# A fused four-layer block: exponential before copy in ScalarE's order of the first attention layer

## The chip, the cores and the metric

One Trainium2 chip, one of its cores. A core has TensorE (matmuls, into the PSUM banks), VectorE, ScalarE and GpSimd (elementwise work; ScalarE has the exponential), and SyncE, which here only issues transfers. Each engine works off its own list of instructions in order and waits at semaphores for the others. The metric is the device time of one execution of the whole kernel in microseconds (us); lower is better. Three runs of a kernel give a median.

## The reference, cut to what matters

The whole function is a block of four layers over x of 32 sequences x 128 tokens x 128 features, each an attention layer and a feed-forward layer with a gated residual. The change touches the first attention layer alone, which has 16 query heads of 8 features and values shared in groups:

```python
def _L0_xattn_ref(x, adj, Wq, bq, Wk, bk, Wv, bv, Wo, bo):
    q = x @ Wq + bq
    k = adj @ Wk + bk
    v = adj @ Wv + bv
    q = q.reshape(b, t, N_HEADS, D_HEAD).transpose(0, 2, 1, 3)
    k = k.reshape(b, v_len, GROUP, D_HEAD).transpose(0, 2, 1, 3)
    v = v.reshape(b, v_len, GROUP, D_HEAD).transpose(0, 2, 1, 3)
    weight = jnp.einsum('bhtd,bgvd->bhtv', q, k) / math.sqrt(D_HEAD)
    weight = jax.nn.softmax(weight, axis=-1)
    out = jnp.einsum('bhtv,bgvd->bhtd', weight, v)
    out = out.transpose(0, 2, 1, 3).reshape(b, t, N_HIDDEN)
    return out @ Wo + bo
...
x = x + jnp.tanh(g_xattn[0]) * _L0_xattn_ref(_layernorm(x, axis=-1), ctx_1024, ...)
```

## The kernel before, in words

The 32 sequences go through a layer in 8 chunks of 4 (`NC = 8`, `CB = 4`). In the first attention layer (`heads0`, one function of that name in each engine's program) a chunk is 8 steps (`STEPS0`), w = 0 to 7. A step takes one unit: 8 (head, sequence) score blocks of 128 x 128, that is two PSUM banks. The order of each engine's instructions is written out by hand: each engine's `body(c, p, more, first, live)` loops over the steps and emits, at fixed lags (`LAG0`), the work of this unit and of earlier ones. Nothing reorders it; semaphores alone tie the engines together.

What happens to unit v, and in which step each engine does it:

- TensorE, step v: scores into banks 0 and 1 (L918). It waits until VectorE has read the scores of the unit before (`A0_less_max`).
- VectorE, step v: the maximum of each row (L2075), then scores minus maximum into the buffer `ex` (L2078, tile `att`), which counts up `A0_less_max`. `ex` has two halves, taken in turn.
- ScalarE, step v: the exponential in place in `ex` (shown as L1485), which counts up `A0_exp`. It waits for `A0_less_max`.
- TensorE, step v+1: eight transposes of `ex` into banks 2 and 3 (L947), which count up `A0_pT_full`. They wait for the exponential and, as there is one pair of banks, for the copy of unit v-1 (`A0_pT`).
- ScalarE, step v+1: the copy of banks 2 and 3 into `pT0` (128x1024, shown as L1483 with tile `arena`), which counts up `A0_pT`. `pT0` holds four units.
- TensorE, in odd steps: the values matmul (L929) of the tile of two units of which the second is v = w-2. It stands after the scores and before the transposes. It waits for `A0_pT` of both units and for `A0_oT`, that is for a small copy (`oT0`, 128x128) that ScalarE makes in even steps behind the big one.
- Then, for the tile: ScalarE copies the result (`outT0`, 128x512, at the end of even steps), TensorE transposes it back (L971), VectorE divides by the sums (L2086, L2087), TensorE transposes again (L936), ScalarE copies to `oT0`, TensorE projects (L961, odd steps), and VectorE adds the residual once a chunk (L2127, step 5).

Beside this the queries, keys and values of the next chunk are prepared in eight pieces (`piece`, `SLICES0 = (0, 0, 1, 4, 5, 6, 6, 7)` gives the step of each). TensorE makes a piece in one PSUM bank, ScalarE copies it out and gives the bank free (`A0_slice_gone`). A step's first piece stands early in the step on both engines (on ScalarE ahead of all else), a second one (steps 0 and 6) late. GpSimd splits keys and queries into bf16 parts in between (L641 to L645).

ScalarE's step before the change is thus: first piece, copy of unit w-1 to `pT0`, copy to `oT0` (even steps), second piece, exponential of unit w, copy to `outT0` (even steps).

The first chunk is followed by a setup of weights for later layers on all engines; chunks 1 to 4 run in a hardware loop, 5 to 7 are written out, and six steps of draining follow chunk 7, which has no pieces (there is no next chunk). The first layer's feed-forward part begins in the drain.

Of the kernel before, what the change touches and what calls it, by code (L numbers as in the profile page):

```python
# [30 lines left out]
STEPS0 = 2 * CB  # L31
# [35 lines left out]
CRED = QUARTERS + 1  # L67
# [42 lines left out]
def slices_at(w):  # L110

    return [s for s, at in enumerate(SLICES0) if at == w]
# [12 lines left out]
def lagging(c, p, w, what, first, live):  # L125

    lag = LAG0[what]
    if w >= lag:
        return (c, p, w - lag) if live else None
    return None if first else (c - 1, 1 - p, w - lag + STEPS0)  # L130


def tile_of(unit, odd=0):

    return (unit[0], unit[1], unit[2] // 2) if unit and unit[2] % 2 == odd else None


def flamingo(nc, a, out):
    ctx = ExitStack()
    with ctx:  # L140
# [5 lines left out]
        def sem(name):  # L146
            if name not in sems:
                sems[name] = ctx.enter_context(nc.semaphore(name))
            return sems[name]
# [7 lines left out]
        def two(i):  # L157
            return banks[:, i:i + 2, :].rearrange("p a (j t) -> p (a j) t", j=CB)

        def slice_bank(s, first):  # L160
            return bank[(6 - s) % 8] if first else bank[6]
# [28 lines left out]
        ex = att[:, 0:2].rearrange("p a s j t -> p (a s) j t")  # L190
# [179 lines left out]
        at = used[0]  # L370
# [1111 lines left out]
        def _(act):  # L1482
            copy = lambda o, i: nc.scalar.activation(o, i, ACT.Copy)  # L1483
            aff = lambda o, i, s, b: nc.scalar.activation(o, i, ACT.Identity, bias=b, scale=s)
            exp = lambda o, i: nc.scalar.activation(o, i, ACT.Exp)  # L1485
            s_held = sem("held")

            def setup():
                act.wait_ge(s_load, 16 * n_loads)
                nc.scalar.activation(gates[:, :], graw[:, :], ACT.Tanh).then_inc(s_setup, 1)  # L1490
# [20 lines left out]
            def heads0():  # L1511
                kA = len(SLICES0)

                def piece(c, p, s, first=False):
                    A = slice_bank(s, first)
                    A16 = A[:, :].bitcast(BF16)
                    act.wait_ge(sem("A0_slice"), c * kA + (s + 1))
                    gone = sem("A0_slice_gone")
                    if s == 0:
                        copy(xnT[:, :], A[:, :]).then_inc(sem("A0_xnT"), 1)  # L1520
                        act.wait_ge(sem("A0_xnT"), c + 1)
                        act.sem_inc(gone, 1)
                        return
                    if s < 3:

                        if s == 1:
                            copy(kvraw0[:, :, :], A[:, 0:CB * KV0].rearrange("p (j d) -> p j d", j=CB)).then_inc(sem("A0_raw"), 1)
                        else:
                            nc.scalar.activation(qraw0[:, :, :], A[:, :].rearrange("p (h d) -> p h d", d=D0), ACT.Copy, scale=float(D0) ** -0.5)\
                                .then_inc(sem("A0_raw"), 1)  # L1530
                        act.wait_ge(sem("A0_raw"), c * 2 + s)
                        act.sem_inc(gone, 1)
                        return
                    if s == 3:
                        for q in range(2):
                            half = slice(q * (P // 2), (q + 1) * (P // 2))
                            i = copy(kT0[half, p, :, q * P:q * P + P], A16[half, 0:W].rearrange("p (j t) -> p j t", j=CB))
                    else:
                        i = copy(qT0[:, p, s - 4, :], A16[:, :])
                    i.then_inc(gone, 1)  # L1540
                    if s == kA - 1:
                        act.wait_ge(gone, c * kA + (kA + 1))
                        act.sem_inc(sem("A0_slices_ready"), 1)

                def body(c, p, more, first=False, live=True):
                    for w in range(STEPS0 if live else DRAIN0):
                        mine = slices_at(w) if more else []
                        for s in mine[:1]:
                            piece(c + 1, 1 - p, s)
                        unit = lagging(c, p, w, "turned", first, live)  # L1550
                        if unit:
                            cc, _, v = unit
                            act.wait_ge(sem("A0_pT_full"), cc * STEPS0 + (v + 1))
                            act.wait_ge(sem("A0_pv_batch"), cc * CB + (v // 2 + 1))
                            at = 2 * v % PT0
                            copy(pT0[:, at:at + 2, :, :].rearrange("p a i t -> p (a i) t"), two(2)).then_inc(sem("A0_pT"), 1)
                        tile = tile_of(lagging(c, p, w, "attended", first, live))
                        if tile:
                            cc, _, j = tile
                            act.wait_ge(sem("A0_oT_full"), cc * (2 * CB) + (2 * j + 2))  # L1560
                            copy(oT0[:, j % 2, :], bank[4 + j % 2][:, 0:P]).then_inc(sem("A0_oT"), 1)
                        for s in mine[1:]:
                            piece(c + 1, 1 - p, s)
                        if live:
                            act.wait_ge(sem("A0_less_max"), c * STEPS0 + (w + 1 + CRED))
                            at = ex[:, w % 2 * 2:w % 2 * 2 + 2, :, :].rearrange("p a i t -> p (a i) t")
                            exp(at, at).then_inc(sem("A0_exp"), 1)
                        tile = tile_of(lagging(c, p, w, "copied", first, live))
                        if tile:
                            cc, _, j = tile  # L1570
                            act.wait_ge(sem("A0_pv_batch"), cc * CB + (j + 3))
                            if j or not isinstance(cc, int) or cc:
                                act.wait_ge(sem("A0_oT_full"), cc * (2 * CB) + (2 * j - 1))
                            copy(outT0[:, :], bank[4 + j % 2][:, :]).then_inc(sem("A0_out"), 1)

                act.sem_inc(sem("A0_slice_gone"), 1)
                act.sem_inc(sem("A0_pT"), CRED)
                act.sem_inc(sem("A0_exp"), CRED)
                act.sem_inc(sem("A0_pv_batch"), 2)
                act.sem_inc(sem("A0_oT"), 2)  # L1580
                for s in range(kA):
                    piece(0, 0, s, first=True)
                body(0, 0, True, True)
                setup()
                with act.Fori(0, NC // 2 - 2) as i:
                    for p in range(2):
                        body(i * 2 + (p + 1), 1 - p, True)
                body(NC - 3, 1, True)
                body(NC - 2, 0, True)
                body(NC - 1, 1, False)  # L1590
                body(NC, 0, False, live=False)
# [1114 lines left out]
```

## Time and profile before

| what | before |
|---|---|
| median of 3 runs | 1580.54 us (1576.93 to 1581.98) |
| profiled execution: its own time, which is its span | 1593.7 us |
| TensorE matmuls busy | 1390.0 us (87%) |
| VectorE busy | 1102.3 us (69%) |
| ScalarE busy | 1016.4 us (64%) |
| mean granted TensorE clock | 0.960 |

The profiled execution is one execution with the profiler on, and the times within it are read from its first instruction. The first attention layer lies between about 35 and 280 us of it. Busy shares are means over a span in which stages with different limits follow each other; what holds for the stage of the change is read from its own stretch.

### The profile page before, as it was taken

To read this page: it belongs to the slowest core of one execution; us is meant where nothing else is said; L and a number is where in the kernel's file an instruction comes from. 1 tells how busy PE (TensorE), PEld (TensorE's weight loads), DVE (VectorE), ACT (ScalarE), POOL (GpSimd) and SP (SyncE) were. 2 spreads that over 40 slices of the span, in tenths; PEclk is the share of its full clock that TensorE was granted. 3 is DMA by queue.
4 is the path that set the end of the run, shared out by engine and by line. 5 is a ranking of instruction groups with operands and counts; after the bars stand their busy time and mean duration, and the time that the engine had idled before them with its cause. 6 is when DMAs were issued, how large, how long until landed. Compare 5 with 4: busy or idle time off the path is not lost.

```text
span 1593.7 us, 35101 instructions
## 1 busy us (share of the span) xinstructions
PE 1390.0 (87%) x9982; PEld 1034.7 (65%) x9982; DVE 1102.3 (69%) x3531; ACT 1016.4 (64%) x2931; POOL 533.7 (33%) x631
## 2 busy tenths in 40 slices
PE   4788887998898987998999989999986299999994
PEld 3566665676644465443666666666665299999994
DVE  4788877787777666884567767777675556666665
ACT  2688886554555564224887867877864277777762
POOL 3353566222211411000002242342243445554550
PEclk9999999999999999999999999999998599999998
DMA  8000059400499910000000010010034122222227
GB/s 194 24 8 7 14 93 178 69 0 14 96 179 179 136 34 21 0 0 7 1 8 23 13 36 18 18 34 11 18 133 156 37 62 66 67 66 65 63 57 264
DMA packets 143417, 98.35 MB, mean 62 GB/s; under 512 B 20595, under 2 KB 132510, under 8 KB 142150
## 3 DMA queue, kind: packets, MB, share of 16 engines
q1 hardware_dynamic: 134598, 80.08, 25.2%
q0 software_dynamic: 8704, 16.87, 3.2%
q8 instruction: 55, 0.90, 0.2%
q14 instruction: 60, 0.49, 0.1%
HBM read 43.03 MB, written 54.93 MB: 61 GB/s over the span
## 4 chain that ended last, share of the span: by engine, by line
PE 59%; DVE 13%; ACT 12%; issue 11%; another core or an unknown queue 2%; DMA 1%; DVEq 1%; SPq 1%; POOL 0%; ACTq 0%; POOLq 0%
PE bank L1450 7%; PE bank L1442 7%; PE bank L1006 6%; PE bank L1022 4%; ACT arena L1483 3%; PE bank L947 3%; PE bank L1294 3%; PE bank L1057 3%; ACT att L1620 3%; PE bank L1010 2%; PE bank L1042 2%; ACT att L1485 2%; PE bank L1032 2%; PE bank L1370 2%
## 5 line engine op out<-in xcount | busy, mean ns | idle before, releaser
L1483 ACT ACTIVATE arena<-bank 128x512 f32<-128x512 f32 (+7 forms) x380 | 245.6, 675 | 150.4 <-PE bank L1357 53.9
L1902 ACT ACTIVATE att<-bank,arena 128x128 f32<-128x128 f32 x576 | 165.0, 371 | 70.0 <-PE bank L1442 65.8
L820 POOL DMA_INDIRECT expert_outputs<-arena x144 | 145.1, 1007 | 146.6 <-issue 100.8
L1620 ACT ACTIVATE att<-bank,arena 128x128 f32<-128x128 f32 x512 | 180.7, 395 | 17.1 <-DVE arena L2160 14.6
L774 POOL DMA_INDIRECT dispatched_rows<-arena x112 | 113.8, 1016 | 181.2 <-DVE arena L2049 115.3
L608 POOL TENSOR_TENSOR ve<-mv,eps 128x4 f32<-128x4 f32 x64 | 13.0, 203 | 425.9 <-DVE mv L1965 416.9
L1450 PE MATMUL bank<-arena,att 128*128 128x128 f32 x1152 | 153.5, 276 | 2.3 <-ACT att L1902 1.7
L1442 PE MATMUL bank<-xnT,arena 128*128 128x128 f32 x1152 | 154.0, 277 | 0.4 <-ACT xnT L1483 0.4
L1450 PEld LDWEIGHTS bank<-arena,att 128*128 128x128 f32 x1152 | 140.1, 192 | 4.8 <-ACT att L1902 4.8
L1442 PEld LDWEIGHTS bank<-xnT,arena 128*128 128x128 f32 x1152 | 141.6, 194 | 1.0 <-ACT xnT L1483 1.0
L1483 ACT ACTIVATE xnT<-bank 128x128 f32<-128x128 f32 (+1 forms) x180 | 63.5, 353 | 90.9 <-PE bank L841 43.1
L1620 ACT ACTIVATION_READ_ACCUMULATOR att<-bank,arena 128x1 f32 x512 | 120.2, 235 | 0.0
L2632 DVE COPY arena<-arena 128x512 f32 x144 | 62.3, 433 | 82.9 <-issue 81.6
L2160 DVE TENSOR_REDUCE arena<-bank 128x4 f32<-128x512 f32 x128 | 82.3, 685 | 45.4 <-PE bank L1022 45.3
L1605 ACT ACTIVATE arena<-bank 128x512 f32<-128x512 f32 x128 | 76.0, 613 | 58.1 <-PE bank L1006 50.8
L947 PE MATMUL bank<-ident,att 128*128 128x128 f32 x512 | 70.9, 283 | 31.7 <-ACT att L1485 31.5
L1022 PE MATMUL bank<-arena 64*128 64x128 f32 x1024 | 79.7, 292 | 18.3 <-issue 7.4
L2075 DVE TENSOR_REDUCE nmx<-bank 128x8 f32<-128x1024 f32 x64 | 78.0, 1219 | 25.4 <-PE bank L918 24.9
L2174 DVE COPY arena<-bank 128x512 f32<-128x512 f32 x64 | 44.0, 687 | 72.4 <-PE bank L1042 38.1
L1022 PEld LDWEIGHTS bank<-arena 64*128 64x128 f32 x1024 | 66.5, 193 | 40.6 <-issue 31.6
L2166 DVE TENSOR_TENSOR att<-att,arena 128x512 f32<-128x512 f32 x128 | 89.0, 695 | 4.4
L1294 PE MATMUL bank<-arena 128*128 128x512 f32 x192 | 89.4, 603 | 0.0
(375 smaller groups left out, 3257.0 us busy)
## 6 DMA issues: line engine op xcount, KB each, us to landing
dispatched_rows<-padf SPq DMA_DIRECT2D x16, 2128.5 KB, 31.8
arena<-dispatched_rows SPq DMA_DIRECT2D x144, 64.5 KB
cxT<-in_ctx SPq DMA_DIRECT2D x32, 256.0 KB
arena<-in_L_ffn_w SPq DMA_DIRECT2D x8, 1024.0 KB
arena<-expert_outputs SPq DMA_DIRECT2D x8, 1024.0 KB, 13.8
expert_outputs<-arena POOLq DMA_INDIRECT x144
out_x<-x SPq DMA_DIRECT2D x8, 256.0 KB, 4.9
dispatched_rows<-arena POOLq DMA_INDIRECT x112
```

What stands on the lines that cost most here:

```text
L774: pl.indirect_dma_start(sent, bass.IndirectOffsetOnAxis(places[:, q:q + 1], 0), held[:, q, :], None)\
L820: pl.indirect_dma_start(sent_out, bass.IndirectOffsetOnAxis(xtu3[:, s, P:P + 1], 0), yt3[:, s, :], None, bounds_check=TOP3 * TOKENS - 1, o ...
L947: last = nc.tensor.transpose(bank[2 + k][:, i * P:i * P + P], ex[:, v % 2 * 2 + k, i, :], ident[:, :])
L1006: last = nc.tensor.matmul(A[:, :], wqk3[:, t, pair * P:pair * P + P], cxT[:, p, :] if t else xnT[:, :], start=True, stop=True)
L1022: last = nc.tensor.matmul(bank[side][:, i * P:i * P + P], q, k, start=True, stop=True)
L1294: last = nc.tensor.matmul(bank[1 + j][:, :], xsT1[:, p * CB + j, t:t + P], wconv1[:, t, :], start=False, stop=(t == 2))
L1442: last = nc.tensor.matmul(bank[s % 2][:, k * P:k * P + P], w1c3[:, s % 4, k * P:k * P + P], xnT[:, (s % 4) * P:(s % 4) * P + P], start=Tru ...
L1450: last = nc.tensor.matmul(bank[2 + s % 2][:, 0:P], h3[:, s % 2, k * P:k * P + P], w2c3[:, s % 4, k * P:k * P + P], start=(k == 0), stop=(k ...
L1483: copy = lambda o, i: nc.scalar.activation(o, i, ACT.Copy)
L1620: last = nc.scalar.activation(ex3_of(w, side)[:, i, :], bank[side][:, i * P:i * P + P], ACT.Exp, bias=nm3[:, w % 2, h:h + 1], accum_out=su ...
L1902: last = nc.scalar.activation(h3[:, s % 2, k * P:k * P + P], bank[s % 2][:, k * P:k * P + P], ACT.Gelu, bias=b1c3[:, s % 4, k:k + 1])
L2166: v.tensor_tensor(ex3_of(w, side), ex3_of(w, side), rs3[:, w % 2, side:2 * HQ:2].unsqueeze(2).to_broadcast([P, HQ, P]), ALU.mult) .then_in ...
```

## The change

In ScalarE's `body` of `heads0` the exponential of unit w goes from behind the second piece to directly behind the first piece, ahead of the copy of unit w-1. Its wait for VectorE goes with it. Nothing else is touched. ScalarE's step is then: first piece, exponential of unit w, copy of unit w-1 to `pT0`, copy to `oT0` (even steps), second piece, copy to `outT0` (even steps).

```diff
                         for s in mine[:1]:
                             piece(c + 1, 1 - p, s)
+                        if live:
+                            act.wait_ge(sem("A0_less_max"), c * STEPS0 + (w + 1 + CRED))
+                            at = ex[:, w % 2 * 2:w % 2 * 2 + 2, :, :].rearrange("p a i t -> p (a i) t")
+                            exp(at, at).then_inc(sem("A0_exp"), 1)
                         unit = lagging(c, p, w, "turned", first, live)
                         if unit:
...
                         for s in mine[1:]:
                             piece(c + 1, 1 - p, s)
-                        if live:
-                            act.wait_ge(sem("A0_less_max"), c * STEPS0 + (w + 1 + CRED))
-                            at = ex[:, w % 2 * 2:w % 2 * 2 + 2, :, :].rearrange("p a i t -> p (a i) t")
-                            exp(at, at).then_inc(sem("A0_exp"), 1)
                         tile = tile_of(lagging(c, p, w, "copied", first, live))
```

## Rows read from the trace of the kernel before

**Rows 1.** The page, part 5: the group of the transposes of unit v

```profile
L947 PE MATMUL bank<-ident,att 128*128 128x128 f32 x512 | 70.9, 283 | 31.7 <-ACT att L1485 31.5
```

**Rows 2.** Busy time by stretch: a loaded chunk, and the setup

```profile
core 0: us, PE busy (x) PEld busy (x) DVE busy (x) ACT busy (x) POOL busy (x), PEclk, DMA share, GB/s
129.04:158.29 29.25, 24.49 (x214) 18.18 (x215) 24.00 (x38) 24.59 (x34) 14.20 (x14) 1.00 0.03 9
62.00:72.00 10.00, 6.48 (x33) 5.98 (x33) 7.34 (x20) 2.24 (x6) 0.00 (x0) 0.66 0.00 0
```

**Rows 3.** Timeline of one loaded chunk: start us, us, engine, line, tiles, count

```profile
129.42 1.22 DVE L2078 TENSOR_TENSOR att<-bank,nmx 128x1024 f32<-128x1024 f32 x1
...
131.78 1.07 PE L929 MATMUL bank<-arena 128*32 128x512 f32 x8
...
134.65 0.39 PE L961 MATMUL bank<-wo,arena 128*128 128x128 f32 x2
...
134.87 0.60 PE L918 MATMUL bank<-arena 128*128 128x256 bf16 x4
...
136.77 1.23 DVE L2078 TENSOR_TENSOR att<-bank,nmx 128x1024 f32<-128x1024 f32 x1
...
136.95 1.09 PE L947 MATMUL bank<-ident,att 128*128 128x128 f32 x8 [1.37 <-ACT att L1485]
...
138.08 1.19 ACT L1483 ACTIVATE arena<-bank 128x1024 f32<-128x1024 f32 x2 [1.18 <-PE bank L947]
...
139.16 1.06 ACT L1485 ACTIVATE att<-att 128x1024 f32<-128x1024 f32 x1
...
139.32 1.07 PE L929 MATMUL bank<-arena 128*32 128x512 f32 x8 [0.41 <-ACT arena L1483]
...
140.32 1.09 PE L947 MATMUL bank<-ident,att 128*128 128x128 f32 x8
...
141.25 0.39 PE L961 MATMUL bank<-wo,arena 128*128 128x128 f32 x2
...
141.55 0.61 PE L918 MATMUL bank<-arena 128*128 128x256 bf16 x4
...
142.45 1.05 ACT L1485 ACTIVATE att<-att 128x1024 f32<-128x1024 f32 x1
143.40 2.48 ACT L1483 ACTIVATE arena<-bank 64x512 bf16<-64x512 bf16 x4
143.46 1.22 DVE L2078 TENSOR_TENSOR att<-bank,nmx 128x1024 f32<-128x1024 f32 x1
...
145.92 1.07 PE L929 MATMUL bank<-arena 128*32 128x512 f32 x8 [0.41 <-ACT arena L1483]
...
150.73 1.23 DVE L2078 TENSOR_TENSOR att<-bank,nmx 128x1024 f32<-128x1024 f32 x1
...
152.89 1.07 PE L929 MATMUL bank<-arena 128*32 128x512 f32 x8
...
153.88 0.45 PEld L903 LDWEIGHTS bank<-ident,arena 128*128 128x128 bf16 x8 [0.84 <-ACT arena L1483]
...
154.75 1.09 PE L947 MATMUL bank<-ident,att 128*128 128x128 f32 x8 [0.24 <-ACT att L1485]
...
158.74 1.22 DVE L2078 TENSOR_TENSOR att<-bank,nmx 128x1024 f32<-128x1024 f32 x1
```

**Rows 4.** Timeline of chunk 7, which has no pieces

```profile
246.47 1.23 DVE L2078 TENSOR_TENSOR att<-bank,nmx 128x1024 f32<-128x1024 f32 x1
...
266.06 1.22 DVE L2078 TENSOR_TENSOR att<-bank,nmx 128x1024 f32<-128x1024 f32 x1
...
272.56 0.86 PEld L947 LDWEIGHTS bank<-ident,att 128*128 128x128 f32 x8 [1.10 <-ACT att L1485]
```

**Rows 5.** Timeline of chunk 0 and the start of chunk 1

```profile
41.44 1.22 DVE L2078 TENSOR_TENSOR att<-bank,nmx 128x1024 f32<-128x1024 f32 x1
...
54.21 1.22 DVE L2078 TENSOR_TENSOR att<-bank,nmx 128x1024 f32<-128x1024 f32 x1
...
71.38 1.23 DVE L2078 TENSOR_TENSOR att<-bank,nmx 128x1024 f32<-128x1024 f32 x1
...
73.20 1.06 PE L929 MATMUL bank<-arena 128*32 128x512 f32 x8
```

## Prediction

> **What bounds the kernel now.** I read the page first, then the stretches, then the timeline of one chunk, engine against engine. The page's costliest groups name one wait of this stage: TensorE's transposes of the probabilities (L947) stood 31.7 us idle, 31.5 of it for the exponential [rows 1]. So the exponential is the last thing before the transposes. The reader is to see next that no engine is full: in a chunk of 29.25 us TensorE is busy 24.5, VectorE 24.0 and ScalarE 24.6 us, at a granted clock of 1.00 [rows 2]. The stage is therefore bound by chains that go from engine to engine, and the question is which chains pass through ScalarE's order.
>
> I call M(w) the moment at which VectorE has subtracted the maximum in step w (end of L2078), T(w) the eight transposes of unit w, which TensorE issues in its step w+1, and PV the values matmul (L929), which stands in TensorE's queue in odd steps between the scores and T. Two loops run side by side in the timeline [rows 3]. The first: T(w-1), copy, exponential, T(w). In the step after 136.95 that is 1.09 for T, 0.04, copy to exponential 1.08 (138.08 to 139.16, with the small copy of oT0 behind it) and 1.06 for the exponential. The second: scores 0.60, maximum, subtraction 1.22, next scores, since the scores may overwrite their banks only after M. They are of one length. M(2) is 136.77 + 1.23 = 138.00, and the transposes beside it end at 136.95 + 1.09 = 138.04. ScalarE takes the copy at 138.08 and the exponential at 139.16; both inputs were there at 138.0 in truth. From that instant ScalarE has two pieces of work, and the change only swaps them.
>
> **What each one releases.** T(w) needs both: the exponential as its input, the copy because it writes the banks that the copy reads. For T(w) it doesn't matter which comes first. PV needs the copy alone (and in these steps the small copy of oT0, which follows it), and PV is ahead of T in TensorE's queue. Today PV runs while ScalarE does the exponential: it starts at 139.32, T at 140.32 the moment it has been issued. After the change ScalarE's copy comes second, PV starts only after both, and its 1.00 us and all that is queued behind it (piece, T, projection, the next scores, VectorE's maximum and subtraction) come later. That is a wait added to the path that sets the stage's period.
>
> **The price of one pair of steps.** After M of an even step: release 0.04 (138.04 to 138.08), exponential 0.95 (142.45 to 143.40, start to start), the big copy and that of oT0 together 1.19 (138.08, x2), release 0.05 (139.27 to PV at 139.32). PV starts 2.23 after M. Where it starts now, all from [rows 3]:
> - steps 0 and 1: M at 129.42 + 1.22 = 130.64, PV 131.78, 1.14 behind; the chain behind it is TensorE's queue, then scores, maximum, subtraction. Later by 1.09.
> - steps 2 and 3: M 138.00, PV 139.32, 1.32 behind; 0.91 later. The scores behind it waited a little for VectorE: they follow the projection by 0.22 elsewhere (134.65, 134.87), by 0.30 here (141.25, 141.55), so 0.08 is absorbed. Later by 0.83.
> - steps 4 and 5: M 143.46 + 1.22 = 144.68, PV 145.92, 1.24 behind. Later by 0.99.
> - steps 6 and 7: M 150.73 + 1.23 = 151.96, PV 152.89. Here the next piece waited 0.84 for another copy of ScalarE's (153.89), and T came at 154.75, 2.79 behind M. In the new order that copy follows the one of oT0 and ends about 3.1 behind M, under PV, which is through after its 1.00 at 3.23; the piece takes 0.45, T comes at 3.68. Later by 0.89.
>
> Together 3.80 us a chunk: 29.25 becomes about 33.05. The six chunks 1 to 6 make 22.8.
>
> **The edges.** Chunk 7 carries no pieces of a next chunk. Its three pairs from 246.47 to 266.06 take 19.59 [rows 4]. A bare pair comes out in the new order as 2.23 + 1.00 (PV) + 1.15 (T and the projection up to the scores: 140.32 to 141.47 without the 0.08) + 0.60 + 2.53 (scores' end to M: 134.87 + 0.60 to 138.00) = 7.51, the third with some 0.35 for the residual, which waits for the projection: 22.9, or 3.3 more. The last T (272.56, 5.28 behind M(6)) needs both results after the copy of outT0 and comes some 0.6 later. Chunk 0: two pairs between 41.44 and 54.21 take 12.77 [rows 5]; without projection and, at first, without oT0 the new pairs are about 7.1 and 7.5: 1.8 more. Its last pair runs into the setup, for which ScalarE has to finish the same two pieces in either order: nothing. In chunk 1, M(0) is 71.38 + 1.23 = 72.61 and PV 73.20, just 0.59 behind, since the copy had been made during the setup: 0.55 more than counted. Sum: 22.8 + 3.9 + 1.8 + 0.55 = 29.0 us.
>
> **What is moved, and what is queued behind it.** No instruction is added, removed or resized, and none of those moved issues a DMA. The exponential's wait for VectorE now stands ahead of the big copy, the copy of oT0 and, in steps 0 and 6, the second piece's copy. Behind them wait PV, the next T (banks 2 and 3), the projection, the pieces of TensorE that need the slice bank free, and through PV GpSimd's split of the next chunk's keys and queries. That split ends early enough: its queries are wanted at step 5, in a chunk that is itself 3.8 us longer. SP's loads of the context wait for a TensorE piece and are used one chunk later. Where the trace shows no such order the bounds are these: below, a gain if M comes well ahead of the end of T (next part); above, 2.23 - 0.59 = 1.64 for each of the 31 PVs concerned (0.59 being the earliest place of PV in the rows [rows 5]), 51 us. I take the sum, since each term is read at its own place in a chunk.
>
> **A rule weighed.** The rows say that TensorE's transposes are kept waiting by the exponential, 31.5 us in all [rows 1]. By that alone, an exponential issued first should win. The Trainium skill says so in general: Perfetto Trace Analysis, section "Identifying Performance Opportunities" (Optimization Strategy), finds the gaps of the bounding engine, asks which semaphore ends them, and has that dependency start sooner. Applied to this wait it speaks for the change, and would bring the time of the first rival below. The trace does not bear it out here, because what is put off in exchange releases the same engine.
>
> **The rivals.**
> 1. Faster: the exponential hides under the transposes. If M(w) came at least 0.95 before T(w-1) ended, ScalarE would do the exponential during T, and T's loop would be 1.09 + 0.04 + 1.02 + 0.04 = 2.2 us; the scores and VectorE's loop would bound, about 2 us a chunk less: 1580.5 - 16 = 1565. It decides at that lead. The lead is 0.04 at M(2) [rows 3]. Chance 0.04.
> 2. No change, 1578 to 1584: PV's delay is eaten by slack. This needs under 0.15 us per PV where I count 0.83 to 1.09; the slack that I find is 0.08. Chance 0.04.
> 3. Half the loss: the exponential, done earlier, lets loaded steps (copies of pieces) catch up by some 0.4 per pair, 31 x 0.45 = 14: 1594, at most 1600. For it: ScalarE is idle 4.7 us of 29.25. Chance 0.11.
> 4. Larger: even steps lose too, because ScalarE, standing at the exponential, takes up the copy late when VectorE runs behind T (maximum late by the residual or the norm). Some 0.45 more per step over 56 steps: +54, 1635. Against it: M and the end of T lie 0.04 apart in the step shown, and a late M delays the next scores in either order. Chance 0.06.
> 5. The clock falls. With setup's idle TensorE the granted clock was 0.66 over ten microseconds [rows 2], which is a mix of the 2.4 and the 1.2 GHz level. If the longer waits did that to this stage, PV, T, projection and scores of each pair (about 2.7 us) would double: 31 x 2.7 more, about 1693. Waits such as the 1.37 ahead of T at 136.95 [rows 3] stand in a chunk at 1.00 today; the new ones are some 1.6 us. Chance 0.03. The Trainium skill has such a rule (TensorE: Matmul & The Clock Gate, section "HAM oscillation"): idle gaps put the engine back to half rate; no run here yet shows it for gaps of this size.
>
> **How the numbers follow.** The profiled execution's own time is its span, 1593.7 us; the timed runs have a median of 1580.5, 13.2 below, and the difference lies around the stage, not in it. So the span should be about 1622.7, and the median 1580.5 + 29.0 = 1609.5. Forecast 0.72. Its own range is 1603 to 1615: plus or minus a fifth of the sum. To leave out no more than two in ten, the range goes down to 1596, into the third rival, and up to 1618; the far cases 1, 2, 4 and 5 stay outside. About 0.3%, some 5 us, is what a measurement of this kernel can tell from no change. Faster 0.04 (rival 1), same 0.04 (rival 2), slower 0.92 (the others).
>
> **What would show it.** In the changed profile the exponential starts within 0.1 us of the end of L2078's subtraction and the idle time before it is put down to VectorE. The wait of PV for ScalarE's copy grows to over 1 us in nearly every odd step; T in odd steps no longer waits for the exponential but stands right behind PV or its piece. A chunk lasts 33 us, a bare pair 7.5 us. The waits of VectorE's maximum for the scores grow by about the same sum. The granted clock stays 1.00 and everything after the first attention layer is only shifted. I am wrong if PV does not wait longer, if the exponential often ends before T does, or if the chunk is under 31 us.

## The result, and the profile after

The changed kernel takes 1615.81 us (median of 5 runs, 1611.49 to 1617.82); the kernel before, run beside it, 1580.26 us (1576.93 to 1581.98). The ratio is 1.0218, with a 95% interval of 1.0201 to 1.0236: slower by 35.5 us. The forecast was 1609.5 in a range of 1596 to 1618.

The profiled execution of the changed kernel has a span of 1611.8 us, that of the kernel before 1593.7. These two spans must not be subtracted. I take as the layer's end the first matmul with the gate weights of the feed-forward part (L1118). It stands here in the trace of before:

```profile
282.20 1.84 PE L1118 MATMUL bank<-xnT,wg 128*128 128x512 f32 x2
```

and here after the change:

```profile
314.82 2.05 PE L1118 MATMUL bank<-xnT,wg 128*128 128x512 f32 x2
```

From there to the end the execution of before took 1311.5 us, the changed one 1297.0, and the executions of the experiments below 1291 to 1298 with the same code in that part. The profiled execution of before was a long one, by 15 us, in stages that the change does not touch. What can be compared is the layer: its end moved from 282.20 to 314.82, by 32.6 us.

Groups by line, from 30 to 320 us of the changed kernel; the columns are count, busy us and mean ns, then idle time of the engine ahead of them and what ended it. L947 are the transposes T, L1485 is the exponential, L929 the values matmul PV:

```profile
L947 PE MATMUL bank<-ident,att 128*128 128x128 f32 x512 | 69.8, 281 | 26.0 <-ACT arena L1483 26.0
L1485 ACT ACTIVATE att<-att 128x1024 f32<-128x1024 f32 x64 | 67.5, 1055 | 38.3 <-DVE att L2078 36.3 <-ACT arena L1483 0.7 <-ACT arena L1529 0.4
...
L929 PE MATMUL bank<-arena 128*32 128x512 f32 x256 | 35.0, 617 | 44.6 <-ACT arena L1483 44.6
```

The same view of the kernel before, for the two lines not shown there yet (T is in [rows 1]):

```profile
L1485 ACT ACTIVATE att<-att 128x1024 f32<-128x1024 f32 x64 | 67.5, 1055 | 1.9 <-DVE att L2078 1.1 <-ACT arena L1483 0.2
...
L929 PE MATMUL bank<-arena 128*32 128x512 f32 x256 | 34.1, 603 | 8.4 <-ACT arena L1483 8.2
```

Three readings. PV waited 8.2 us for ScalarE's copy (tile `arena`, L1483) and now waits 44.6. The exponential, which waited for nothing (1.9), now stands 36.3 us at VectorE's subtraction, that is at the head of ScalarE's list with the copy behind it. T waited 31.5 us for the exponential and now 26.0 for the copy, which has become the second of the two: the wait that the swap removes comes back under another name.

The timeline of one loaded chunk of the changed kernel, which answers to [rows 3]:

```profile
141.75 1.22 DVE L2078 TENSOR_TENSOR att<-bank,nmx 128x1024 f32<-128x1024 f32 x1
...
143.01 1.06 ACT L1485 ACTIVATE att<-att 128x1024 f32<-128x1024 f32 x1 [1.33 <-DVE att L2078]
...
143.98 1.29 ACT L1483 ACTIVATE arena<-bank 128x1024 f32<-128x1024 f32 x3
...
145.20 1.06 PE L929 MATMUL bank<-arena 128*32 128x512 f32 x8 [1.15 <-ACT arena L1483]
...
150.19 1.23 DVE L2078 TENSOR_TENSOR att<-bank,nmx 128x1024 f32<-128x1024 f32 x1
...
151.44 1.06 ACT L1485 ACTIVATE att<-att 128x1024 f32<-128x1024 f32 x1 [1.29 <-DVE att L2078]
...
152.41 1.17 ACT L1483 ACTIVATE arena<-bank 128x1024 f32<-128x1024 f32 x2
...
153.63 1.07 PE L929 MATMUL bank<-arena 128*32 128x512 f32 x8 [1.40 <-ACT arena L1483]
...
154.63 1.09 PE L947 MATMUL bank<-ident,att 128*128 128x128 f32 x8
...
157.68 1.22 DVE L2078 TENSOR_TENSOR att<-bank,nmx 128x1024 f32<-128x1024 f32 x1
...
161.26 1.06 PE L929 MATMUL bank<-arena 128*32 128x512 f32 x8 [1.69 <-ACT arena L1483]
...
166.06 1.23 DVE L2078 TENSOR_TENSOR att<-bank,nmx 128x1024 f32<-128x1024 f32 x1
...
169.51 1.06 PE L929 MATMUL bank<-arena 128*32 128x512 f32 x8 [1.18 <-ACT arena L1483]
...
174.91 1.22 DVE L2078 TENSOR_TENSOR att<-bank,nmx 128x1024 f32<-128x1024 f32 x1
```

M(0) is 141.75 + 1.22 = 142.97. The exponential follows at 143.01, the copies at 143.98, PV at 145.20: 2.23 us behind M, as worked out. M(2) = 151.42, exponential 151.44, copies 152.41, PV 153.63, 2.21 behind, T at once behind PV at 154.63. From M(2) to M(4) (158.90) it is 7.48 us; the prediction had 7.51, the kernel before 6.68. The next M(0) is at 176.13, a chunk of 33.16 us against a predicted 33.05.

VectorE's maximum (L2075), which the prediction also named, waited 24.9 us for the scores before and now waits 50.2:

```profile
L2075 DVE TENSOR_REDUCE nmx<-bank 128x8 f32<-128x1024 f32 x64 | 78.0, 1219 | 51.3 <-PE bank L918 50.2 <-DVE wsc L1957 0.3 <-DVE stats L2093 0.2
```

Busy time in this chunk (answers to [rows 2]) and in a stretch of chunk 1:

```profile
core 0: us, PE busy (x) PEld busy (x) DVE busy (x) ACT busy (x) POOL busy (x), PEclk, DMA share, GB/s
142.97:176.13 33.16, 24.32 (x216) 18.10 (x216) 24.15 (x38) 24.70 (x33) 14.19 (x14) 1.00 0.03 8
74.00:84.00 10.00, 8.02 (x43) 5.79 (x44) 4.99 (x10) 5.46 (x8) 5.17 (x9) 0.66 0.07 21
```

In the chunk the engines do the same work as before (24.3, 24.2 and 24.7 us) in 33.16 us instead of 29.25, at a granted clock of 1.00. In chunk 1 the clock was at 0.66 over ten microseconds. The matmuls there, in the changed kernel:

```profile
76.17 1.94 PE L929 MATMUL bank<-arena 128*32 128x512 f32 x8 [1.55 <-ACT arena L1483]
78.04 2.08 PE L890 MATMUL bank<-wq,xnT 128*128 128x128 f32 x8
79.91 1.91 PE L947 MATMUL bank<-ident,att 128*128 128x128 f32 x8
81.61 0.53 PE L961 MATMUL bank<-wo,arena 128*128 128x128 f32 x2
```

PV waited for ScalarE's copy until 76.17 and then lasted 1.94 us, at the 1.2 GHz level, and the piece and the transposes behind it were slow too. The granted clock had come back to 1.00 behind the setup and fell again before PV started: it was 1.00 from 74 to 75 us, 0.53 from 75 to 76 and 0.50 from there to 81.5. In the profiled execution of before PV of that place took 1.06 us [rows 5]. That is not a matter of the order alone, as e3_last3 shows below.

### The profile page after: what moved, and what is told of

It reads as the page before. It is cut to its first block, busy times and chain, and to the rows that moved or that the text cites. A ratio compares the mean times of both kernels' runs of the same rounds, so it can differ in the third digit from the quotient of the medians.

```text
span 1611.8 us, 35078 instructions
## 1 busy us (share of the span) xinstructions
PE 1386.6 (86%) x9959; PEld 1035.5 (64%) x9982; DVE 1103.5 (68%) x3531; ACT 1015.3 (63%) x2931; POOL 533.6 (33%) x631
## 4 chain that ended last, share of the span: by engine, by line
PE 63%; DVE 14%; ACT 11%; issue 8%; DMA 1%; POOL 1%; DVEq 1%; SPq 1%; ACTq 0%; POOLq 0%
PE bank L1006 7%; PE bank L1450 7%; PE bank L1442 7%; PE bank L1022 4%; ACT arena L1483 4%; PE bank L1057 4%; PE bank L1294 3%; ACT att L1620 3%; PE bank L1042 3%; PE bank L1010 3%; PE bank L1032 3%; PE bank L929 2%; PE bank L947 2%; DVE att L2078 2%; DVE nmx L2075 2%
## 5 line engine op out<-in xcount | busy, mean ns | idle before, releaser
L1483 ACT ACTIVATE arena<-bank 128x512 f32<-128x512 f32 (+7 forms) x380 | 244.2, 672 | 142.5 <-PE bank L1357 55.5
L1483 ACT ACTIVATE xnT<-bank 128x128 f32<-128x128 f32 (+1 forms) x180 | 63.6, 353 | 85.4 <-PE bank L841 42.6
L2075 DVE TENSOR_REDUCE nmx<-bank 128x8 f32<-128x1024 f32 x64 | 78.0, 1219 | 51.3 <-PE bank L918 50.2
L947 PE MATMUL bank<-ident,att 128*128 128x128 f32 x512 | 69.8, 281 | 26.0 <-ACT arena L1483 26.0
L1485 ACT ACTIVATE att<-att 128x1024 f32<-128x1024 f32 x64 | 67.5, 1055 | 38.3 <-DVE att L2078 36.3
## 6 DMA issues: line engine op xcount, KB each, us to landing
dispatched_rows<-padf SPq DMA_DIRECT2D x16, 2128.5 KB, 34.6
```

The lines of the kernel that those rows point to most:

```text
L947: last = nc.tensor.transpose(bank[2 + k][:, i * P:i * P + P], ex[:, v % 2 * 2 + k, i, :], ident[:, :])
L2075: step(v.tensor_reduce(nmx0[:, w % 2, :], two(0), AX, ALU.max))
```

## The experiments

Each was run in five or more rounds beside the kernel before, whose median was 1580.2 us beside e1 to e4, 1581.2 beside h1, h2, l1 and l2, and 1580.0 beside the others. "Chunk" is the time from M(0) to the next M(0) in the profiled execution, as read for chunk 3 (which keeps the old order in e3_last3); "layer's end" the start of the first L1118 matmul, as above.

| kernel | median us | ratio, 95% interval | chunk us | layer's end us |
|---|---|---|---|---|
| before | 1580.3 | | 29.3 | 282.2 |
| changed | 1615.8 | 1.0201 to 1.0236 | 33.2 | 314.8 |
| e1_even | 1611.1 | 1.0192 to 1.0224 | 33.2 | 316.1 |
| e2_odd | 1581.2 | 1.0000 to 1.0019 | 29.3 | 283.6 |
| e3_last3 | 1593.5 | 1.0073 to 1.0103 | 29.3 | 299.1 |
| e4_again | 1615.0 | 1.0212 to 1.0244 | 33.2 | 315.3 |
| h1_bf16_before | 1572.0 | 0.9931 to 0.9967 | 28.5 | 276.7 |
| h2_bf16_after | 1598.4 | 1.0085 to 1.0130 | 31.1 | 304.0 |
| l1_late_before | 1614.4 | 1.0195 to 1.0237 | 35.1 | 317.3 |
| l2_late_after | 1618.6 | 1.0227 to 1.0266 | 36.0 | 321.1 |
| e5_between | 1604.7 | 1.0140 to 1.0172 | 32.3 | 307.3 |
| b1_oT_first | 1578.4 | 0.9985 to 1.0003 | 29.1 | 281.2 |
| l3_before | 1580.5 | 0.9999 to 1.0016 | 29.6 | 283.5 |
| l4_after | 1586.0 | 1.0036 to 1.0067 | 30.3 | 290.1 |

**Half of the steps: e1_even and e2_odd.** The new place of the exponential is used in even steps only (e2_odd has `w % 2 == 1` in both conditions):

```diff
+                        if live and (w % 2 == 0):
+                            act.wait_ge(sem("A0_less_max"), c * STEPS0 + (w + 1 + CRED))
...
+                            exp(at, at).then_inc(sem("A0_exp"), 1)
                         unit = lagging(c, p, w, "turned", first, live)
...
-                        if live:
+                        if live and not (w % 2 == 0):
```

> The exponential goes ahead of the copy in ScalarE's even steps alone (w = 0, 2, 4, 6); odd steps keep the old order. My theory: the loss comes from the values matmul, which stands in TensorE's odd steps and is released by the copy that ScalarE makes in the even step before. So this half of the change carries all of the loss: about 1614 us (1610 to 1617), as the full change. Rival (each step loses the same, because ScalarE stands at the exponential while the copy could be made): half the loss, about 1598.

> The other half: exponential first in odd steps alone. The copy of an odd step releases no values matmul, only the next transposes, which need both results in either order. My theory: no change against the kernel before, 1577 to 1584 us. Rival (each step loses the same): about 1598.

Measured: 1611.1 for the even steps, all but some 4 us of the loss and with an interval that overlaps that of the full change; and its layer ends at 316.1, no earlier than in the changed kernel. The odd ones take 1581.2, 0 to 3.0 us above the kernel before by the interval. The rival that every step loses alike (1598 for both) is out. In e1_even the groups read:

```profile
L947 PE MATMUL bank<-ident,att 128*128 128x128 f32 x512 | 71.0, 283 | 30.9 <-ACT att L1485 30.9
...
L929 PE MATMUL bank<-arena 128*32 128x512 f32 x256 | 35.0, 617 | 42.5 <-ACT arena L1483 42.5
```

and in e2_odd:

```profile
L947 PE MATMUL bank<-ident,att 128*128 128x128 f32 x512 | 70.1, 281 | 32.7 <-ACT arena L1483 31.3 <-ACT att L1485 1.0
L1485 ACT ACTIVATE att<-att 128x1024 f32<-128x1024 f32 x64 | 67.7, 1057 | 9.0 <-DVE att L2082 6.3 <-ACT arena L1483 0.9 <-ACT arena L1529 0.4
...
L929 PE MATMUL bank<-arena 128*32 128x512 f32 x256 | 34.1, 603 | 8.3 <-ACT arena L1483 8.2
```

PV waits 42.5 us in the one and 8.2 in the other. In e2_odd T's wait has gone over to the copy (31.3) as in the changed kernel, and costs next to nothing: its sum is 32.7 us, where [rows 1] has 31.7.

**The last three chunks: e3_last3.** The condition on the order is that the chunk is 5, 6 or 7.

> The change in chunks 5, 6 and 7 alone. By the prediction's terms a chunk costs 3.8 us (two of them) and chunk 7 3.9: about 11.5 us, so 1592. If the loss were made mostly at the start (setup and the clock in chunk 1) it would be under 8: 1587 or less.

Measured: 13.3 us more, 11.5 to 16.3 by the interval. That is some 4.4 us to each of the three chunks, so the loss is spread over the chunks. In the profiled execution chunk 6 was 33.3 us long, chunk 5, in which the granted clock fell once, 34.9.

This trace also holds a comparison for chunk 1, which has the old order here. PV of that place waited for nothing and was slow all the same:

```profile
73.67 1.84 PE L929 MATMUL bank<-arena 128*32 128x512 f32 x8
```

Chunk 1 took 30.4 us in it, and 30.1 in b1_oT_first, where the profiled executions of before and e2_odd have 28.8. So the lower clock at the start of chunk 1 comes in the old order too, in some executions, and costs about 1.5 us there.

**The changed kernel once more: e4_again.**

> The changed kernel again, on the same chip as the other three: 1611 to 1618 us. In its trace I look at chunk 1: if the clock fell to 1.2 GHz there once more, after the setup, the first pair of steps of chunk 1 takes about 11 us from subtraction to subtraction; if not, about 8.4.

Measured: 1615.0. The first pair of chunk 1 took 9.9 us, between the two values that I gave (11.1 in the first execution). Chunk 1 took 34.6 us here and 35.9 in the first execution. In the trace of before it took 28.8; with the 3.80 of a chunk and the 0.55 of this place the forecast makes it 33.1. Here the granted clock had not come back at all behind the setup: it was 0.51 from 66 to 79 us, so PV's wait did not bring it down. And the clock fell a second time in the middle of the layer, in chunk 6. TensorE's matmuls there:

```profile
252.61 1.06 PE L929 MATMUL bank<-arena 128*32 128x512 f32 x8 [1.57 <-ACT arena L1483]
253.61 1.09 PE L947 MATMUL bank<-ident,att 128*128 128x128 f32 x8
...
257.94 0.61 PE L918 MATMUL bank<-arena 128*128 128x256 bf16 x4
260.34 1.62 PE L929 MATMUL bank<-arena 128*32 128x512 f32 x8 [1.78 <-ACT arena L1483]
261.88 1.03 PE L903 MATMUL bank<-ident,arena 128*128 128x128 bf16 x8
262.71 1.73 PE L947 MATMUL bank<-ident,att 128*128 128x128 f32 x8
```

PV waited 1.57 us for the copy at 252.61 and then ran in 1.06; it waited 1.78 us at 260.34, lasted 1.62, and what follows runs at the lower level (T 1.73 in place of 1.09); the granted clock was 0.50 from 261 to 264. That chunk took 34.9 us, 1.6 more than chunk 5 before it. In the first execution of the same kernel PV of the same place waited as long, and the clock stayed:

```profile
261.04 1.06 PE L929 MATMUL bank<-arena 128*32 128x512 f32 x8 [1.78 <-ACT arena L1483]
```

**A shorter values matmul: h1_bf16_before, h2_bf16_after.** PV reads only the upper halves of its operands, so its result is less precise than the reference's; all else stays.

```diff
-  nc.tensor.matmul(bank[4 + j % 2][rows0, :], v0[:, pp, j, :], pT0[:, ...].rearrange("p i t -> p (i t)"), ...)
+  hi = lambda t: t.bitcast(BF16).rearrange("p (n two) -> p n two", two=2)[:, :, 1]
+  nc.tensor.matmul(bank[4 + j % 2][rows0, :], hi(v0[:, pp, j, :]), hi(pT0[:, ...].rearrange("p i t -> p (i t)")), ...)
```

> The old order, with the values matmul made shorter: it reads only the upper 16 bits of each probability and value (as bf16), so its precision is less. It lasts 1.0 us now; I expect 0.3 to 0.5. Alone it should gain little, since in bare steps the exponential ends the wait of the transposes anyway: 1570 to 1580 us.

> The new order with the same shorter values matmul. My theory: what the new order exposes is the values matmul and the pieces behind it, so a bare pair costs only as much more as the matmul lasts (0.3 to 0.5 us where it was 0.83 to 1.1), loaded pairs keep most of their loss, and the difference to the run before falls from 35 us to some 20 to 27. Rival (ScalarE standing at the exponential costs by itself, whatever the values matmul lasts): the difference stays at 33 to 36.

PV in the old order with the short matmul:

```profile
L930 PE MATMUL bank<-arena 128*32 128x512 bf16 x128 | 13.3, 405 | 6.0 <-ACT arena L1484 5.6
```

and in the new order:

```profile
L930 PE MATMUL bank<-arena 128*32 128x512 bf16 x128 | 13.4, 406 | 45.3 <-ACT arena L1484 45.3
```

Four matmuls of 405 ns overlap to 0.41 us in a step, where the long form took 1.07:

```profile
218.18 0.41 PE L930 MATMUL bank<-arena 128*32 128x512 bf16 x4 [1.78 <-ACT arena L1484]
```
 The swap now costs 1598.4 - 1572.0 = 26.4 us in place of 35.5, at the upper end of what I gave (20 to 27) and clear of the rival's 33 to 36, though PV waits as long as in the changed kernel (45.3). So the price goes with how long PV lasts and not with how long it waits. Chunk 3 takes 31.1 us against 28.5, 2.6 more, where the long form had 3.8. The 26.4 are in part the clock: in the profiled execution of h2_bf16_after it fell in chunks 5, 6 and 7 (32.4 and 34.0 us for chunks 5 and 6, 31.1 for the chunks 2 to 4), in that of h1_bf16_before in none of them. The one timed run of each with a mean granted clock of 0.963 took 1591.3 and 1571.8 us, 19.5 apart.

**PV taken away from ScalarE's pair: l1_late_before, l2_late_after.** PV goes one step later in TensorE's list, to even steps, where the copy that it needs is a whole step old; the copy to `outT0` goes to the start of ScalarE's next even step.

```diff
-LAG0 = {"turned": 1, "values": 2, "copied": 2, "back": 4, ...}
+LAG0 = {"turned": 1, "values": 3, "copied": 4, "back": 4, ...}
```

> The old order of copy and exponential, with the values matmul one step later in TensorE's queue (even steps, a lag of 3 in place of 2), where the copy that it needs was made a whole step before; ScalarE's copy of its result goes to the start of the next even step. By my theory the wait of 0.41 us that it has today goes, but even steps hold two pieces of the next chunk on TensorE as well: 1570 to 1585 us.

> The same with the exponential first in every step. My theory: nothing on TensorE but the next transposes waits for the copy any more, and they need both results in either order. So the swap costs 0 to 5 us against the run before (up to the bound 1590). Rival (the order itself costs, by ScalarE standing at the exponential): 30 us or more, 1605 and above.

The first expectation failed: 1614.4, not 1570 to 1585. I had left GpSimd out. It writes the next chunk's values when the last PV of the chunk before is done, and only then splits the queries, and that PV now came a step later. The chain of waits of l1_late_before names it (engine, line and tile that waited, what for: us in total, times, longest):

```profile
PE bank L903 <- POOL arena L645: 30.6, 6, 5.3
```

TensorE's clock went down behind each of these stalls (0.93 over 105 to 316 us), which adds to the loss. The swap cost 4.2 us on top, but beside a stall of 5 us in each chunk this could be cover, so the pair doesn't settle the question by itself.

**The same, mended: l3_before, l4_after.** GpSimd writes the values after it has split the queries.

```diff
-                if more:
-                    pl.wait_ge(sem("A0_pv_batch"), c * CB - 2)
                 pl.wait_ge(sem("A0_raw"), c * 2 + 1)
-                pl.tensor_tensor(v0[:, p, :, 0:D0], ...)
...
-                pl.tensor_tensor(third, ...).then_inc(sem("A0_split"), 1)
+                step(pl.tensor_tensor(third, ...))
+                pl.wait_ge(sem("A0_pv_batch"), c * CB - 2)
+                pl.tensor_tensor(v0[:, p, :, 0:D0], ...).then_inc(sem("A0_split"), 1)
```

> The late values matmul (lag 3) with the old order, mended: GpSimd writes the next values after it has split the queries, so that its wait for the last values matmul no longer holds up the piece of step 5 (that wait was 5.7 us in each chunk of l1_late_before). A chunk of 35.0 us should come down to about 29.5: 1578 to 1590 us.

> The same with the exponential first. My theory: the swap costs 0 to 6 us against l3_before, since no values matmul waits for the copy behind the exponential; it can't be hidden by the stall of step 5 any more. Rival (the order itself costs): 30 us or more above l3_before.

Measured: 1580.5 in the old order, 1586.0 in the new: the swap costs 5.5 us where it cost 35.5. This is the decisive pair. T (L949 here) and PV (L931) in l3_before:

```profile
L949 PE MATMUL bank<-ident,att 128*128 128x128 f32 x512 | 69.1, 279 | 21.3 <-ACT att L1487 21.3
...
L931 PE MATMUL bank<-arena 128*32 128x512 f32 x256 | 35.0, 619 | 0.0
```

and in l4_after:

```profile
L949 PE MATMUL bank<-ident,att 128*128 128x128 f32 x512 | 68.4, 277 | 19.0 <-ACT arena L1485 18.6
...
L931 PE MATMUL bank<-arena 128*32 128x512 f32 x256 | 35.0, 619 | 0.0
```

PV waits for nothing in either, and T's wait only changes its name, from the exponential to the copy. Most of the remaining 5.5 us (6.6 at the layer's end in the traces) sits in the last pair: from M(7) to M(0) it is 4.75 in l4_after and 4.09 in l3_before. There another instruction of TensorE is released by ScalarE's copies: the piece of step 7 (L905), which stands ahead of T(6) and needs the bank that the copy of step 6's second piece frees. That copy, too, now stands behind the exponential. In l3_before the piece started 1.95 us behind M(6) (152.55):

```profile
154.50 0.62 PE L905 MATMUL bank<-ident,arena 128*128 128x128 bf16 x8 [0.50 <-ACT arena L1485]
```

and in l4_after 3.13 us behind M(6) (155.40):

```profile
158.53 0.62 PE L905 MATMUL bank<-ident,arena 128*128 128x128 bf16 x8 [1.70 <-ACT arena L1485]
```

Over the layer the pieces' waits for such copies went from 5.2 to 13.0 us. No run takes this piece away, so that it makes up the rest is read from the traces and not tried. A smaller part is the copy of T: T(5) ends 0.31 us ahead of M(6) in l4_after, and ScalarE, standing at the exponential, can't use the gap.

**The exponential between the two copies: e5_between.** Order: big copy, exponential, copy of oT0.

> ScalarE's order is: big copy, exponential, small copy of oT0. The values matmul waits for both copies. My theory counts to the later one: release 0.04, big copy 0.92, exponential 0.95, small copy 0.28, release 0.05, the same 2.23 us behind the subtraction, so the loss is nearly the full one: 1608 to 1617 us. If only the big copy mattered, the order would be as good as the old: 1578 to 1584.

Measured: 1604.7, 24.7 us more than before, less than the 28 to 37 that I gave. That the small copy alone, put late, makes such a loss confirms that PV waits for both. Where the rest went is seen in steps 7 to 1 of a loaded chunk:

```profile
137.63 1.09 PE L947 MATMUL bank<-ident,att 128*128 128x128 f32 x8 [0.39 <-ACT att L1485]
138.09 1.23 DVE L2078 TENSOR_TENSOR att<-bank,nmx 128x1024 f32<-128x1024 f32 x1
...
138.84 1.02 ACT L1483 ACTIVATE arena<-bank 128x1024 f32<-128x1024 f32 x1 [0.84 <-PE bank L947]
...
139.76 1.05 ACT L1485 ACTIVATE att<-att 128x1024 f32<-128x1024 f32 x1
...
140.71 0.38 ACT L1483 ACTIVATE arena<-bank 128x128 f32<-128x128 f32 x2
...
141.03 1.07 PE L929 MATMUL bank<-arena 128*32 128x512 f32 x8 [0.59 <-ACT arena L1483]
```

T ends at 137.63 + 1.09 = 138.72, M(0) is at 139.32. The big copy is started at 138.84, in that gap, so PV starts at 141.03, 1.71 behind M and not 2.23. The changed kernel can't use the gap, because ScalarE stands at the exponential until M. A chunk is 32.3 us long, 0.9 shorter than in the changed kernel.

**A small gain sought: b1_oT_first.** The old order with the copy of oT0 ahead of the big copy.

> The old order with the small copy of oT0 ahead of the big copy. Its input is ready before the transposes end, while ScalarE waits, so the values matmul starts up to 0.2 us earlier in each pair of steps. At most 0.2 x 31 = 6 us; in bare pairs the exponential ends the wait of the transposes 0.05 later anyway, so rather 0 to 4: 1576 to 1581 us.

Measured: 1578.4, ratio 0.9985 to 1.0003. A chunk in the trace is 0.3 us shorter (29.06 against 29.32), but the whole is no difference that this measurement can tell. None of the kernels that keep the computation beats the kernel before measurably; the short values matmul does, by 8 to 9 us, at the price of precision.

## Why the prediction was right

**The mechanism** was right for what costs the time. Exponential and copy release the same transposes, so their order means nothing to T (e2_odd: no change); the copy alone releases PV, which stands ahead of T, and that is where the loss is (e1_even: nearly all of it; l3_before and l4_after: 5.5 us left once PV doesn't wait there). What is left goes for the most part through another copy, that of a piece, which the prediction had counted in steps 6 and 7 only as hidden under PV.

**The price of a pair** was right within 0.12 us: M(0) to M(2) takes 8.45 us in the changed kernel and 7.36 in the kernel before, M(2) to M(4) 7.48 and 6.68, M(4) to M(6) 8.39 and 7.28, M(6) to M(0) 8.84 and 8.00. That is 1.09, 0.80, 1.11 and 0.84 more, where 1.09, 0.83, 0.99 and 0.89 were forecast. (The predicted chunk of 33.05 starts from a stretch of 29.25 us; from M(0) to M(0) a chunk of before takes 29.32, which makes it 33.12, against 33.16 measured.) Chunks 2 to 6 together lost 19.6 us (19.0 forecast), chunk 0 lost 1.4 (1.8), and from M(0) of chunk 7 to the layer's end it was 4.5 in the first execution and 4.1 in e4_again (3.9).

**The size was 6.5 us low**, 29.0 against 35.5 (31.8 to 37.3 by the interval). The term that was mis-sized is the clock. I had rival 5 as a fall for the whole stage, at 0.03, and put nothing for a short one into the sum. In the layer the loss is 32.6 us in the first profiled execution and 33.1 in e4_again, so 3.6 to 4.1 above the forecast. Of that, chunk 1 makes 2.8 and 1.5 us, and chunk 6 of e4_again 1.6. This is measured against a trace of before in which chunk 1 happened to show no fall, and in which such a fall would have cost about 1.5 us (e3_last3, b1_oT_first).

The timed runs say the same without the traces. The changed kernel's five have mean granted clocks of 0.956 to 0.963 and a median of 0.958; the 51 of the kernel before that ran beside the experiments have 0.959 to 0.967 and a median of 0.963. At 0.963 the changed kernel took 1611.5 us (one run) and the kernel before 1580.0 (the median of 13); at 0.964 e4_again's run took 1608.2 and the kernel before 1578.0 to 1578.4. At like clocks the loss is thus some 30 to 31.5 us, 1 to 2.5 above the forecast, and the other 4 or so go with the clock. The mean is one over the whole program, so this is a rough split. The measured median lies within the range, but the sum had no term for that part.

Why the clock falls more often in the new order is open. Apart from l1_late_before and l2_late_after, with their stall of 5 us in each chunk, every trace in which it fell within chunks 2 to 7 has the new order there: chunk 5 of e3_last3, chunk 6 of e4_again, three chunks of h2_bf16_after. In e3_last3 and e4_again the fall stands at a PV that had waited 1.78 us; the same wait left it up in the first execution. At the start of chunk 1 it comes in the old order too. No experiment was made on the clock itself.

**The rivals.** Rival 1 (the exponential hides under T) and rival 2 (slack eats the delay) are out; the slack was the 0.08 us counted. Rival 3 (half the loss) is out by e1_even. Rival 4, the copy taken up late because ScalarE stands at the exponential, exists in small: it is what e5_between saves (PV 1.71 us behind M in place of 2.23, 0.9 us a chunk), and a small part of the 5.5 us of l4_after against l3_before. In my count it was part of the 2.23 us from M, so it needed no term. In odd steps it costs next to nothing (e2_odd). Rival 5, the clock, did not come as a fall for the whole stage, but it came in short. The rule of the Trainium skill (Perfetto Trace Analysis, "Identifying Performance Opportunities") held in its first half, since the exponential did start sooner, and not in its outcome: the wait of T went from 31.5 to 26.0 us [rows 1], and PV's grew by 36.4.

**What the profile was to show** came true for the exponential right behind M, PV's wait over 1 us, a chunk of 33 us and a bare pair of 7.5 (7.58 in chunk 7). VectorE's maximum waits 25.3 us longer for the scores, where about 29 were given. It failed in two points: the granted clock did not stay at 1.00, and the span was another. I expected 1622.7 by adding the sum to the span of before, holding its 13.2 us above the median for something constant. The changed kernel's span lies 4 us below its median. That excess was the one execution's, in later stages. It does no harm to the forecast, which was added to the median.

## What to carry to other kernels

In this kernel, and it is worth a look in others: when one engine has two pieces of work ready at once and both end the same wait, their order is set by what else each one releases: the one with more queued behind it on other engines goes first, even if the profile puts the costliest wait down to the other. Find that out from the in-order lists (what stands ahead of the waiting instruction on its engine, and for what that waits), and count the new place of each released instruction from the moment at which both inputs are there. A later place of one instruction also moves what waits for its buffers on an engine that looks idle; leaving GpSimd out cost 5 us a chunk in l1_late_before.

## What the runs showed of the hardware that was not expected

The granted clock fell to the 1.2 GHz level in the middle of loaded chunks: in chunk 6 of e4_again and in chunk 5 of e3_last3, each time within 1 us of the start of a PV that had waited 1.78 us, and for some 3.4 us (PV 1.62 us in e4_again instead of 1.06). Whether it fell differed between executions of one kernel: in the first execution of the changed kernel PV waited 1.78 us twice (chunks 5 and 6) and the clock stayed at 1.00 (over 109 to 314 us). Behind the setup it fell a second time, or had not come back yet, in both orders: PV lasted 1.94 us after a wait of 1.55 in the changed kernel, and 1.84 us after none in e3_last3, where that chunk has the old order. Behind the stalls of 5 us in l1_late_before it fell in every chunk. The Trainium skill (TensorE: Matmul & The Clock Gate, section "HAM oscillation") ties the fall to idle gaps of the engine. The falls in the loaded chunks agree in that they stand behind PV's wait; the rows do not show that one such gap alone decides it.
